# Fused AdaLN block on one Trainium2 core: weights laid out by the host, set-up loads on two queues, one routing mask for both experts

## What is computed

```python
x = x + ga * attn(layernorm(x) * (1 + ca) + sa)     # ga, ca, ...: rows of silu(c) @ wmod
x = x + gb * ffn(layernorm(x) * (1 + cb) + sb)

# attn: 16 heads of width 16, causal linear attention with random features
phi = exp(q @ omega - |q|^2 / 2) / sqrt(128)        # k likewise, 128 features
y   = einsum(phi_q, cumsum(phi_k v)) / (einsum(phi_q, cumsum(phi_k)) + 1e-6)
out = y @ W_proj + b_proj

# ffn: 4 experts that share Wi (1024x256) and Wo, and differ by a rank 4 term; top 2 of 4
w   = top-2 weights of softmax(x @ Wg.T + bg)
h_e = relu(x @ Wi.T + (x @ A_e.T) @ B_e.T)
out = sum_e w_e * (h_e @ Wo.T)
```

## Time and profile before

| | us |
|---|---|
| median of 3 runs | 768.58 (768.09 to 769.23) |
| the profiled execution, its own time | 768.62 |
| its span, first to last instruction | 766.8 |
| PE busy in the span | 737.7 (96%) |
| DVE busy | 524.4 (68%) |
| ACT busy | 427.7 (56%) |
| POOL busy | 68.4 (9%) |

### The profile page before, as it was taken

How to read it: one execution, slowest core, us unless ns; L and a number is a source line. 1 busy time by engine, 2 the same in 40 slices (tenths; PEclk the granted TensorE clock), 3 DMA queues, 4 the chain that set the end, 5 groups by cost and what they waited for, 6 DMA issues and landing times.

```text
span 766.8 us, 17051 instructions
## 1 busy us (share of the span) xinstructions
PE 737.7 (96%) x6138; PEld 601.8 (78%) x6138; DVE 524.4 (68%) x1273; ACT 427.7 (56%) x777; POOL 68.4 (9%) x88
## 2 busy tenths in 40 slices
PE   4989999999999999999999999999999999999697
PEld 3768878887698878888788877988788876988476
DVE  5466777676775776677865777767766777666566
ACT  3566646674557655665466745575456655655232
POOL 1620110002000020001000020000200010000200
PEclk9999999999999999999999999999999999999899
DMA  8770272105601064102811066000741038100000
GB/s 255 236 130 2 84 188 46 55 0 155 159 14 41 27 197 91 55 0 91 195 29 55 0 169 146 27 27 27 202 85 55 0 108 185 21 29 27 3 1 28
DMA packets 35133, 62.22 MB, mean 81 GB/s; under 512 B 5068, under 2 KB 19172, under 8 KB 35044
## 3 DMA queue, kind: packets, MB, share of 16 engines
q1 hardware_dynamic: 35112, 61.95, 30.5%
HBM read 39.91 MB, written 22.02 MB: 81 GB/s over the span
## 4 chain that ended last, share of the span: by engine, by line
PE 90%; DVE 5%; DMA 2%; ACT 2%; SPq 1%; issue 1%; POOL 0%; ACTq 0%; DVEq 0%; POOLq 0%
PE pa L566 13%; PE prod L579 8%; PE ring L545 6%; PE ring L420 5%; PE pa L420 5%; PE pa L421 5%; PE pa L422 5%; PE ring L421 5%; PE ring L422 5%; PE ring L599 4%; PE pa L679 4%; PE ring L550 3%; PE ring L764 2%; PE ring L606 2%; PE ring L711 2%; PE ring L754 2%
## 5 line engine op out<-in xcount | busy, mean ns | idle before, releaser
L1199 DVE TENSOR_TENSOR am_phk<-pa,const 128x512 f32<-128x512 f32 x112 | 77.0, 688 | 39.2 <-PE pa L566 38.4
L566 PE MATMUL pa<-phq,phkT 128*128 128x128 f32 x768 | 101.2, 275 | 0.0
L566 PEld LDWEIGHTS pa<-phq,phkT 128*128 128x128 f32 x768 | 95.3, 191 | 2.1
L1377 DVE SCALAR_TENSOR_TENSOR am_phk<-ring,am_phk 128x512 f32<-128x512 f32 x64 | 44.1, 689 | 47.2 <-PE ring L764 47.2
L545 PE MATMUL ring<-xq,omega_x 100*128 100x512 f32 x196 | 70.5, 439 | 2.9 <-DVE wo_l L1193 1.4
L420 PE MATMUL pa<-wo_r,qk_r 128*128 128x256 f32 x256 | 72.1, 282 | 0.6 <-DVE qk_l L1382 0.6
L421 PE MATMUL pa<-wo_r,qk_l 128*128 128x256 f32 x256 | 72.0, 281 | 0.0
L422 PE MATMUL pa<-wo_l,qk_r 128*128 128x256 f32 x256 | 71.9, 281 | 0.0
L923 ACT ACTIVATE phq<-ring 128x512 f32<-128x512 f32 x82 | 49.3, 601 | 39.3 <-PE ring L545 38.1
L1001 ACT ACTIVATE qk_r<-phq 128x512 fp32r<-128x512 f32 x64 | 40.5, 633 | 49.9 <-DVE phq L1386 49.9
L923 ACT ACTIVATE phkT<-ring 128x512 f32<-128x512 f32 x98 | 58.3, 595 | 14.8 <-PE ring L545 14.5
(11 more groups left out here) (219 smaller groups left out, 1616.7 us busy)
## 6 DMA issues: line engine op xcount, KB each, us to landing
xq<-qk_parts SPq DMA_DIRECT2D x45, 512.0 KB
qk_parts<-qk_r SPq DMA_DIRECT2D x32, 256.0 KB, 3.5
qk_parts<-qk_l SPq DMA_DIRECT2D x32, 256.0 KB, 3.7
xr<-in_L_attn_x SPq DMA_DIRECT2D x8, 512.0 KB, 3.4
out_x<-tg SPq DMA_DIRECT2D x16, 256.0 KB, 2.2
tok<-in_L_attn_x SPq DMA_DIRECT2D x7, 512.0 KB, 3.4
xq<-qk_parts SPq DMA_DIRECT2D x6, 256.0 KB
phq<-in_L_wmod SPq DMA_DIRECT2D x2, 512.0 KB, 7.5
```

The source lines that it names most:

```text
L566: mm = pe.matmul(score_bank(q, a)[:, tt], phkT[:, q % 2, a, tt], query(q)[:, a, tt], start=True, stop=True)
L1199: dve.tensor_tensor(am[:, 2 * (q % 2) + a, :].rearrange("p (c t) -> p c t", c=NT), score_bank(q, a)[:].rearrange("p (c t) -> p c t", c=NT) ...
L1377: dve.scalar_tensor_tensor(r2[:, f % 2, :], z_bank[f % 4][:], 0.0, rho, ALU.max, ALU.mult).then_inc(r2_done.sem, 1)
```

## The change

What it does:

- `laid_out` (in `kernel()`) transposes, repeats and pads the weights on the host: Wi and Wo come as columns, A and Wg as one padded tile `low_columns`, B as `lora_rows` (96 x 1024), omega with its norm rows as one 100 x 256 tile, `cT` and the q/k bias as columns. The 42 PE transpositions of weights are gone, with their PSUM copies; `low_t` is loaded directly.
- ACT issues four loads (first part of `wmod`, `W_attn`); SP issues the others.
- ACT and DVE split Wi and Wo from SBUF in pieces 1024 wide; `setup_wi` moves on ACT ahead of `front_qk` and on DVE ahead of `split_qk`.
- On PE, `norms(0, 0)` and `qk(0, 3)` go ahead of `setup_gate(0)`, `setup_mods(1)` goes behind `norm_split`, and `values` goes ahead of the lead tiles, which use five PSUM banks where they had three.
- POOL no longer fills `mk1` and `mk2`, and makes `lora_d` and a masked `lora_w` out of the split B (`lora_by_expert`, two instructions of 96 x 1024) behind `gate_projection`.
- Each group of 32 mask columns now holds expert one in its first 16 and the difference in its last 16. One mask is transposed, one product `low_both` is made; `lora_w` has zeros in the rows of the second half, `lora_d` in those of the first.
- On DVE, `router` comes ahead of the subtraction that writes `low`'s rest, and the rows for `rho` are written behind `mask_low`. On PE, the transposition of the logits comes two matmuls earlier, as does that of the masks.

```diff
-        low1, low2 = norm_r[0:LROWS], norm_l[0:LROWS]
-        mk1, mk2 = sb("mk1", [P, NT, LROWS]), sb("mk2", [P, NT, LROWS])
+        low_both = norm_r[0:LROWS]
+        mk = sb("mk", [P, NT, LROWS])
...
-        lead_bank = [ring[RING], pa[0], pa[1]]
+        lead_bank = [ring[RING], pa[0], pa[1], ring[1], ring[2]]
...
-            load(ld_cond, *((cT[:, k, :], cond[:, k * P:(k + 1) * P].rearrange("b p -> p b")) for k in range(KT)))
+            load(ld_cond, (cT[:].rearrange("p k b -> p (k b)"), c_cols))
...
-            load(ld_wi, *((wi_raw[k].rearrange("p (t d) -> p t d", t=FT // 2),
-                           wi.rearrange("(k t p) d -> k p t d", k=2, p=P)[k]) for k in range(2)))
+            load(ld_om, (om_f, omega_rows))
+            load(ld_wi, *((wi_raw[k], wi_t[k * P:(k + 1) * P, :]) for k in range(KT)))
...
             def attend(n, front_next):
                 scores(n, 0, 0)
                 scores(n, 0, 1)
-                pe.wait_ge(late_vec.sem, 10)
+                pe.wait_ge(late_vec.sem, LATE)
...
             def masks(n):
-                for src, need, dst in ((mk1, 18, pa[1]), (mk2, 21, pa[0])):
-                    wait(pe, rt, n, need)
-                    for t in range(NT):
-                        mm = pe.transpose(dst[0:LROWS, t * P:(t + 1) * P], src[:, t, :], ident)
-                    mm.then_inc(mask_ps.sem, 1)
+                wait(pe, rt, n, 21)
+                for t in range(NT):
+                    mm = pe.transpose(pa[1][0:LROWS, t * P:(t + 1) * P], mk[:, t, :], ident)
+                mm.then_inc(mask_ps.sem, 1)
...
                             wait(pe, low_masked, n, 1)
+                            pe.wait_ge(lora_parts.sem, 2)
...
-                        pe.matmul(z_bank[(f - 1) % 4][:], lora_w[:, w], low2, start=False, stop=True,
+                        pe.matmul(z_bank[(f - 1) % 4][:], lora_d[:, w], low_both, start=False, stop=True,
...
             qk(0, 2)
+            norms(0, 0)
+            qk(0, 3)
             pe.wait_ge(set_silu.sem, 4)
             pe.wait_ge(ld_mod[1].sem, 16 * KT)
             setup_gate(0)
-            norms(0, 0)
-            qk(0, 3)
-            setup_mods(1)
-            setup_gate(1)
-            pe.wait_ge(set_mod.sem, 4)
             norms(0, 1)
-            pe.wait_ge(ld_wi.sem, 16 * 2)
-            for q in range(4):
-                setup_wi(q)
-            features(0, 0, range(RUN), lead=True)
-            values(0)
...
+            setup_gate(1)
+            wait(pe, norm_split, 0, 2)
+            setup_mods(1)
+            pe.wait_ge(gates_sb.sem, 1)
+            values(0, [0])
+            pe.wait_ge(gates_sb.sem, 2)
+            values(0, [1])
+            features(0, 0, lead=True)
+            features(0, 1, lead=True)
...
             def ffn_rest(n, front_next):
+                router(n)
                 wait(dve, lg_done, n, 1)
                 wait(dve, low_high, n, 1)
                 dve.tensor_tensor(low[64:96, :].bitcast(F32R), lg[64:96], low[64:96, :], ALU.subtract).then_inc(low_split.sem, 1)
-                router(n)
                 mask_low(n, front_next)
+                ratio(n)
...
+            def lora_by_expert():
+
+                pool.wait_ge(late_vec.sem, LATE)
+                pool.tensor_scalar(lora_d[:], lora_w[:].bitcast(F32), expert[0:LROWS, 1:2], None,
+                                   ALU.mult).then_inc(lora_parts.sem, 1)
+                pool.wait_ge(lora_parts.sem, 1)
+                pool.tensor_scalar(lora_w[:], lora_w[:].bitcast(F32), expert[0:LROWS, 0:1], None,
+                                   ALU.mult).then_inc(lora_parts.sem, 1)
```

More of the change, by code:

```diff
@@ L528, in features @@
                     tile = p * TILES + k
-                    dst = lead_bank[tile % 3] if lead else proj_bank(tile)
+                    dst = lead_bank[tile % 5] if lead else proj_bank(tile)
                     if tile == 0 and lead:
@@ L536, in features @@
                     if tile == 0 and lead:
-                        pe.wait_ge(late_vec.sem, 2)
-                    if lead and tile >= 3:
-                        wait(pe, exp_done, n, tile - 2)
+                        wait(pe, qk_split, n, 4)
+                    if lead and tile >= 5:
+                        wait(pe, exp_done, n, tile - 4)
                     if not lead and 2 <= tile < 2 * TILES:
@@ L681, in projection, with base @@
                     mm.then_inc(prj_ps.sem, 1)
-            def base(n, f, ks=range(KT)):
+            def base(n, f, first=0, last=3 * KT):
                 if f >= 4:
@@ L686, in base @@
                 w = slice(f * P, (f + 1) * P)
-                for k in ks:
-                    if f == 0:
+                for step in range(first, last):
+                    k, term = divmod(step, 3)
+                    if f == 0 and term == 0:
                         wait(pe, h2_parts, n, k + 1)
-                    split3(z_bank[f % 4][:], wi_r[:, k, w], wi_l[:, k, w], h_r[:, k, :], h_l[:, k, :], k == 0, False)
+                    pe.matmul(z_bank[f % 4][:], (wi_r, wi_l, wi_r)[term][:, k, w], (h_r, h_r, h_l)[term][:, k, :],
+                              start=step == 0, stop=False)
             def ffn_head(n, front_next):
@@ L911, in features @@
                     tile = q * TILES + k
-                    bank_of = lead_bank[tile % 3] if lead else proj_bank(tile)
+                    bank_of = lead_bank[tile % 5] if lead else proj_bank(tile)
                     wait(act, proj_ps, n, tile + 1)
```

269 lines of the change are left out of this document (108 added, 161 removed).

## The result

The changed kernel takes **761.25 us** (median of 5 executions, 759.48 to 764.08) where the kernel before takes 768.58 (5 executions, 768.04 to 769.90): a ratio of 0.9916, 95% interval 0.9897 to 0.9934. It is faster by 7.3 us, as the sign was forecast, but the forecast was 12.0 and the time lies 0.75 us above the range.

What follows compares the result with a forecast made beforehand. The prediction took the set-up to be bound by a chain of latencies and the blocks by PE's work. Set-up 9.3 us plus blocks 2.7 made 12.0 off 768.62, a forecast of 756.6 us, range 753.0 to 760.5.

Steps and rivals of the forecast that it cites:

- (1): Set-up, load of x: issued second on SP instead of fourth, landing 1.2 us earlier; bounds nothing or 1.5.
- (5): Set-up, parts returning from DRAM: 3.0 us earlier, so lead tiles start at 32.0; PE ready by 32.1.
- (7): Set-up, PE's stall on the last `wo_l` between first scores and features: goes, 1.4 us less.
- the blocks: Loop blocks: four of eight mask transpositions go; 0.34 us per block, 2.7 in all, bounds 0 and 3.6.
- rival B: Set-up loads come no earlier: x gains nothing, `W_attn` or Wi lands late; 1 us instead of 3, 758.6; chance 0.13.
- (2): Set-up, ACT goes straight from q/k columns to h, 0.7 us; PE starts q and k 1.9 us earlier.
- (3): Set-up, ACT's two roundings of Wi, 16.0 to 18.1, hide before q's first product, by 0.3 us only.
- (4): Set-up, sums of squares ahead of the gate's 1.73 us, near 21.0; norm rest ends 3.2 us earlier, about 24.0.
- (6): Set-up, lead tiles to first scores: 12 exponentials back to back, 6.8 us where 11.7 stood, 4.9 less.
- Rival A: Set-up, DVE and POOL block each other, about 1.6 us per DVE operation; 758 to 761 us; chance 0.22.
- Rival C: Blocks gain nothing because DVE's new order makes PE wait for the mask or ratio; 759.3 us; chance 0.1.
- Rival E: Set-up, lead tiles held by something else, say a second fetch 5 us late; 761.6 us; chance 0.05.

Runs made afterwards that it cites:

- run 4: Changed kernel with all loads on SP's one queue, x ahead of `wmod`; 760.45 us against 761.84 for the changed kernel in the same batch.
- Run 5: Changed kernel with values of tiles 2 and 3 between the lead tiles and 12 unread matmuls keeping PE busy between and behind them; 760.16 us.
- run 9: Changed kernel with the edits of run 4, Run 5, run 6 and run 7 together; 754.80 us, ratio 0.9819 to the kernel before.
- run 11: As run 9 but without the 12 unread matmuls between and behind the lead tiles; 755.34 us, ratio 0.9831 to the kernel before.
- run 2: Changed kernel with unread matmuls on PE between the lead tiles and 7 behind the last; 760.27 us.
- run 7: Changed kernel with DVE splitting the next block's norms ahead of the second half of its values; 761.34 us.
- run 1: Changed kernel measured again, no edit; 761.84 us, ratio 0.990 to the kernel before.
- run 3: Changed kernel's set-up alone: two masks, old order of router and masks, no POOL work on B; 764.67 us, ratio 0.995 to the kernel before.
- run 6: Changed kernel with 31 unread matmuls in PE's seven waits of the last block; 759.02 us.
- run 10: Kernel before the change with the 31 unread matmuls of run 6 in its last block; 764.83 us, ratio 0.9946 to the kernel before.
- Run 8: Changed kernel with POOL starting its gates only after DVE's set-up roundings; read for durations only, single execution 765.15 us.

## Why the prediction was right or wrong

Of the forecast's 12.0 us the medians show 7.3. The steps that failed are (1), the landing of x beside a second queue; (5), where PE's own queue and not the fetch decided the first lead tile, so that it came 1.8 us late (1.05 of it brought along from (1) and (2)); (7), where the clock of the first scores was put at nothing, 1.1 us; the blocks; and the clock of the last block, which has no term at all. Of the missing 4.7 us 2.5 are in the set-up, 0.9 in the blocks and 0.4 outside the span; the last block gave 0.9 more than forecast in this pair of traces, and the medians show 1.8 less than the pair. The sizes below are those of one pair of traces. Between traces of the same set-up the landing of x alone moves by 0.9 to 1.7 us, so a tenth in them is not to be leaned on.

**What bounds the kernel, and the sign: right.** The set-up was the chain of latencies and gave most of what was gained.

**(1) x, 1.2 us forecast: wrong.** x was issued 1.0 us earlier and landed at 7.56 instead of 7.49. The step named what ACT's queue moves beside x and gave nothing and 1.5 us as its bounds, but took 1.2, near the upper one, as if only the issues counted. The lower bound was right: run 4, without that queue, has x at 5.4. This is the first half of rival B, which had a chance of 0.13; its second half, ACT waiting for `W_attn` or Wi, did not come. B's 1 us for steps 1 to 5 is close to the 1.3 measured, but partly by luck, since most of the rest was lost at (5), which B does not name. What came instead was smaller and of another kind: the first half of x had landed before the second, so only two of four statistics (0.76 us, not 1.42) remained behind the landing, and layer norm ended 0.64 us earlier (11.76 against 12.40).

**(2) ACT straight to h, 0.7: mostly covered.** ACT no longer stood in the way, but the transposition (L441) started only at 11.89 and took 1.10, so h began at 13.09, 1.06 earlier than before. PE started q and k at 15.31, 0.95 earlier, where 1.9 was forecast.

**(3) Wi hidden: right,** and with more room: the two roundings ran from 16.46 to 18.47, and ACT then idled 1.1 us.

**(4) Squares ahead of the gate: right in kind,** about 1 us late by (1) and (2): sums at 22.05 (21.0 forecast), the norm rest from 24.13 to 24.8 (24.0).

**(5) Lead tiles at 32.0: the largest error of the set-up.** They came at 33.79. The text had "PE has its values and gates done by 32.1" and gave the fetch as what decides. PE's queue from 22.05 on is 1.05 + 1.6 + 1.73 + 0.98 + 1.93 + 1.68 + 2.9 = 11.9 us without a pause, so it ends near 33.9. From 21.0 to 32.1 the prediction had 11.1; a start 1.05 late and a sum too short by 0.65 turned a near tie into the bound. Run 5 showed it: with half of the values moved behind, the tile came at 32.09 with no wait. The tie was near all the same: in runs 9 and 11 the fetch itself landed only at 33.0.

**(6) Twelve exponentials instead of 11.7 us: right,** 6.5 us instead of the 6.8 forecast.

**(7) The stall: right that it goes, wrong on what follows.** No wait for `wo_l` is left. But scores and features do not stand 2.05 apart but 3.18, at half clock, behind 1.95 us of idle time: 1.1 us over the forecast, and 1.4 over the 1.8 of run 2 at full clock. Of the 42 transpositions that went, the prediction said that they "are not counted again", and it priced nothing for what PE would do in their place. Run 2 shows that matmuls there keep the clock; run 11 shows that the idle time alone does not take it. Sum of the set-up: 6.8 instead of 9.3.

**Margins: right.** The second fetch, `wp_done` (46.9, not 43.0), POOL's two long instructions (2.85 and 2.84 us, from 46.90 to 52.7, inside the 5 to 8 forecast) held nothing up.

**The blocks, 0.34 each: mis-sized.** It is 0.24 where nothing else waits. The masks' transpositions gave what was said, but they began 0.1 us late behind DVE's copies, and the matmul behind the ratio came 0.45 instead of 0.37 after it. In some blocks 0.25 more goes to the return of the norms (run 7), a transfer that the prediction did not price: 1.5 us over seven blocks instead of 2.4.

**Not in the prediction at all:** the last block's clock, in both kernels, and the time outside the span. The medians stand 1.8 us closer than the profiled pair. That the last block's clock is where this went is shown by the traces of runs 1 to 5 (last blocks of 94.6 to 97.3 us against 93.6) and by runs 6 and 10, not by traces of those executions. Outside the span lie 2.23 us instead of 1.76 in the medians, of which one queue instead of two gives 0.17 back; the rest of that stays open.

**Rival A: the mechanism is there, its price was nothing.** The Trainium skill ("SBUF — State Buffer", section "SBUF: two separate sides") describes an exclusive lock: the engine that begins first keeps it for its whole instruction, and the other is blocked. Run 8 bears out that the two engines slow each other (1.23 becomes 2.17 us, 1.93 becomes 2.78), and four of DVE's five operations fit a wait for what was left of POOL's; the fifth does not. It comes to 2.6 us over five operations, where the rival had 1.6 for each, 8 in all: a whole POOL operation each time, where DVE met one part of the way through. DVE ended 2.6 us late and still in time. **Rival C** was right for a part: 0.9 us of the blocks' 2.7 did not come, though by another wait than the two it named. **Rival E** hit the time within 0.4 us by luck: the lead tiles were indeed held by something else, but by 1.8 us and PE's own queue, not by a second fetch 5 us late. **Rival D** did not occur.

## What to carry to other kernels

An instruction that is removed from an engine in a chain of latencies may have been the filling of somebody's wait: look for what idles next, and for what its clock does there, before its time is counted as gained. A load that is issued earlier gains nothing if a second queue moves other bytes beside it: ask what shares the way with it. Where two things end within a microsecond of each other (here PE's queue and a fetch), add up the queue instruction by instruction. And where a wait cannot be removed on an engine whose clock falls when it idles, matmuls that nobody reads cost nothing that shows: here 31 of them in the last block were worth 2 to 4 us, where one mask less gave 1.9.

## What the runs showed of the hardware that was not expected

- The granted clock fell to 0.50 after idle times of PE as short as 1.95 us in the seven traces with the change's order of lead tiles, where PE had 15 matmuls in the 4 us ahead of it (changed kernel's trace), and stayed at 1.00 in run 11 after the same idle time, with 27. In the last block it fell to about 0.5 in the traces of both kernels without filling, not at the same place each time.
- In one execution of the 22 of runs 6, 9, 10 and 11 (run 9's profiled one) the granted clock was 0.95 from 21 us of the span to its end, with 89.33 us a block instead of 88.75 and 759.7 us in all. No row shows why.
- Issuing a transfer 1.0 us earlier did not move its landing (7.56 against 7.49) while another queue moved 1.3 MB beside it; without that queue it landed some 2 us earlier (run 4, at 5.4). The same load landed at 6.60 in run 10's set-up, whose text is that of before: between executions the landing of x moves by 0.9 us, nearly as much as the change was to win there.
- DVE's cast, with one input in SBUF, is slowed by POOL too (0.69 becomes 0.83 and 0.97), not only its operations with two.
